# Attention slots of a fused attention and expert kernel: tasks assigned anew, products in halves

## The chip, the cores and the metric

One core of a Trainium2 chip runs the whole program in one launch. The metric is the time of that launch on the device in microseconds, the median of the runs shown.

## The reference, cut to what matters

Input are 8 sequences of 512 rows of 256 values and one condition vector of 64 values for each. First comes a residual attention with 16 heads of 16 channels:

```
qkv  = x @ Wqkv.T + bqkv;  attn = softmax(q k / 4)
coh  = sigmoid(tanh([x, cond] @ Wc1.T + bc1) @ Wc2.T + bc2)
mod  = attn * coh;  mod /= mod.sum(-1) + 1e-8
fa   = softmax(layernorm(relu(cond @ We1.T + be1) @ We2.T + be2) @ pe.T)
x   += (0.79 * mod + 0.21 * fa) @ v @ Wout.T + bout
```

Then a residual mixture of 8 experts with the two best taken for each row: a gate on the normed row, `h1 = relu(x W1 + b1)`, `h2 = relu(h1 W2 + b2)`, `h2 W3 + b3`, weighed by the gate's softmax.

## The kernel before, in words

Each of the 8 sequences (a batch here) goes through 16 slots: 4 groups of 4 heads, and in a group 4 tiles of 128 keys. A slot s has, in TensorE's program (line 1095):

- `scores(s, (0, 1))`: for two heads a `b_tile` (line 877, the S tile: keys by queries, 512 columns, matmul on line 885) and an `a_tile` (line 863, matmul on line 874) of the slot six ahead. VectorE takes the maxima of the a tiles (`reduce_head`, line 1320), ScalarE the exps of the b tiles (`exps`, line 1203). Three PSUM banks go round for a tiles, two for b tiles, so b tile n waits for the exp of b tile n - 2, and a tile n for the maximum of a tile n - 3.
- `pv(s - 1)`: P times V of the slot before, 8 matmuls in fp32 (line 898), 17 columns wide, for four heads side by side; it waits for all four exps of that slot.
- `scores(s, (2, 3))`.
- `product(t)` (line 959) for each task t that PLAN (line 150) names for the slot. A task is (what, index, batches ahead). `pj` (q and k projections), `c1` (the hidden layer of the coherence) and `v` (values with the gate's inputs, line 971) are six fp16 matmuls each, three for each half e of the channels (`thirds`, line 946, matmul on line 950); x and the weights are split in a high and a low part. `coh` is the coherence (line 1008), `vs` the sum of v over all rows (line 1011), `ot` turns a group's result (line 956), `at` turns half of the channels of the finished attention back, `op` is the output projection, `count` numbers the rows for the experts. Two misc banks alternate over the tasks in the order in which they are issued (`USES`); a task waits until the one before the last is evicted.

The other engines run the same slots in the same order, each in its own queue, and nothing overtakes within one:

- ScalarE (line 1257): exps 0 and 1; in slots 0, 4, 8, 12 `copy_out`, and for the batch before `square_rows` (slots 4 to 7), `send_high` (line 1224, slots 8 and 9) and `weigh`; exps 2 and 3; the evictions of the slot's tasks (`take`, line 1153); in slot 4 `split_x` (line 1146) for the batch after next.
- VectorE (line 1653): the maxima, between them the steps of the routing (`ROUTE_AT`), evictions, `send_low` (slots 8 and 10). At 2, 6, 10, 14 `split_maxima` (line 1322) hands a group's maxima to SP's `store_shift`, which the group's b tiles wait for two slots later.
- GpSimd (line 769): `bias_values` of v tasks and `split_projection` of pj tasks in the slot behind theirs; `fade` (slots 2 and 10), `split_x` (5), `sum_values` (line 671, slot 6, what `vs` needs), gate steps, and `scatter` (line 732): eight indirect DMAs a batch that send the rows to their experts, spread by SCATTER_AT over slot 15 and slots 0, 3, 4 and 6 of the next batch.
- SP (line 560): `write_parts` sends a projection's parts to DRAM (slots 10, 12, 14, 15), `read_stacks` fetches them stacked for the next batch (slots 0, 3, 4).

`send_high` and `send_low` write a finished batch's rows, in two fp16 parts, into the one buffer `sent`, from which `scatter` reads. So `send_high` waits for all scatters of the batches before (line 1227):

```
evicted(act, ("op", r.stop - 1, b))
after(act, scattered, 16 * 2 * TT * b)
```

In the first six batches PLAN's projections are for the batch after next; the last batch has none, and there the expert tables and the first experts' weights are made. From 528 us on the experts run.

Of the kernel before, what the change touches and what calls it, by code (L numbers as in the profile page):

```python
# [9 lines left out]
B, S, E = 8, 512, 256  # L10
# [4 lines left out]
ET = E // P  # L15
# [123 lines left out]
def after(engine, semaphore, count):  # L139
# [10 lines left out]
PLAN = {  # L150
    0: [("coh", 0, 0), ("v", 0, 1)],
    1: [("coh", 1, 0), ("ot", 3, -1)],
    2: [("at", 1, -1), ("coh", 2, 0)],
    3: [("coh", 3, 0), ("op", 0, -1)],
    4: [("op", 1, -1)],
    5: [("ot", 0, 0), ("op", 2, -1)],
    6: [("op", 3, -1)],
    7: [("vs", 0, 0), ("c1", 0, 1)],
    8: [("pj", 0, 2)],
    9: [("ot", 1, 0), ("v", 3, 1)],  # L160
    10: [("pj", 2, 2)],
    11: [("at", 0, 0), ("v", 1, 1)],
    12: [("pj", 1, 2), ("count", 0, -1)],
    13: [("ot", 2, 0), ("pj", 3, 2)],
    14: [("v", 2, 1)],
    15: [("c1", 1, 1)],
# [6 lines left out]

SENT_AT = {8: 0, 10: 1}

SCATTER_AT = {15: (31, 0, 1), 0: (32, 1, 2), 3: (35, 2, 4), 4: (36, 4, 6), 6: (38, 6, 8)}

STACKS_AT = {0: 0, 3: 1, 4: 2}
LEAD = 6
# [41 lines left out]


PROJECTIONS = (0, 2, 1, 3)
PARTS_AT = (10, 12, 14, 15)
WRITES = 16 * 2 * len(PARTS_AT)

# [18 lines left out]
def tasks(s):  # L245

    early = [(what, 0, 0) for what in SETUP_PLAN.get(s, [])]
    here = [(what, i, s // SLOTS + ahead) for what, i, ahead in PLAN[s % SLOTS]]
    return early + [t for t in here if 0 <= t[2] < B]

# [43 lines left out]
def model(nc, ctx, dram, sb, banks, xs, parts_dram, out):  # L294
# [182 lines left out]
    def _(sp):  # L477
# [82 lines left out]
        for s in range(FIRST, LAST):  # L560
            b, at = s // SLOTS, s % SLOTS
            for t in shift_task(s):
                store_shift(*t)
            if s == 1 - SLOTS:
                read_first_stacks()
            elif at in STACKS_AT and 0 < b + 1 < B:
                read_stacks(b + 1, STACKS_AT[at])
            if at == 7:
# [5 lines left out]
                if 0 <= b < B:  # L574
                    sp.dma_start(xr[:, :, 0:E], dram["x"][:, b * TT:(b + 1) * TT, :]).then_inc(xr_in, 16)
            if at in PARTS_AT and 0 <= b + 2 < B:
                write_parts(PARTS_AT.index(at), b + 2)
# [56 lines left out]
    def _(pool):  # L634
# [134 lines left out]
        for s in range(FIRST, LAST):  # L769
# [10 lines left out]
            for t in tasks(s - 1):  # L780
                if t[0] == "v":
                    bias_values(t[1], t[2])
            if at == 5 and 0 < b + 2 < B:
                split_x(b + 2)
            if at == 6 and 0 <= b < B:
                sum_values(b)
# [19 lines left out]
            if at == 13 and 0 <= b - 1 < B:  # L806
                weigh_rows(b - 1)
            if at == 14 and 0 <= b - 1 < B:
                targets(b - 1)
# [53 lines left out]
    def _(pe):  # L863
# [94 lines left out]

        def product(t):
            what, i, b = t  # L960
            side, no = USES[t]
            m = misc[side]
            inputs_ready(t)
            after(pe, misc_read[side], no)
            if what in ("pj", "c1"):
                n = "wc1x" if what == "c1" else "wq" if i < ET else "wk"
                f = slice(i % ET * P, (i % ET + 1) * P)
                for e in range(ET):
                    last = thirds(m[:, :], high[n][:, e, f], low[n][:, e, f], x_high[:, b % 2, e, :], x_low[:, b % 2, e, :],
                                  e == 0, e == ET - 1, False)  # L970
            elif what == "v":
                r = slice(i * P, (i + 1) * P)
                for e in range(ET):
                    last = thirds(m[:, 0:VW], high["wv"][:, e, :], low["wv"][:, e, :], x_high[:, b % 2, e, r],
                                  x_low[:, b % 2, e, r], e == 0, e == ET - 1, True)
# [45 lines left out]
            elif what == "count":  # L1021
                marks = both[:, :, :].rearrange("p t e -> p (t e)")
                nc.tensor.matmul(m[:, 0:TT * NX], tri16[:, :], marks, start=True, stop=True, skip_group_check=True)
                for t2 in range(1, TT + 1):
                    last = nc.tensor.matmul(m[:, t2 * NX:(TT + 1) * NX], ones16[:, :], marks[:, 0:(TT + 1 - t2) * NX],
                                            start=False, stop=(t2 == TT), skip_group_check=True)
            last.then_inc(misc_ready[side], 1)

# [66 lines left out]
        for s in range(FIRST, LAST):  # L1095
            scores(s, (0, 1))
            if scored(s - 1):
                pv(s - 1)
            scores(s, (2, 3))
            for t in tasks(s):  # L1100
                product(t)
            if s == FINAL + 14:
                pe.wait_ge(a_read, B * SLOTS * G)
                hold_ranks(0, EARLY)
                hidden(0, 0, 0, rank_of(0), 1)
# [30 lines left out]
    def _(act):  # L1136
# [120 lines left out]
        for s in range(FIRST, LAST):  # L1257
            b, at = s // SLOTS, s % SLOTS
            if s == -18:
                split_weights("wc1x")  # L1260
                split_weights("wv")
            if scored(s):
                exps(s, (0, 1))
            if at % TT == 0 and scored(s - 1):
                copy_out(s - 1)
            if 4 <= at < 8 and 0 <= b - 1 < B:
                square_rows(at - 4, b - 1)
            if at in (8, 9) and 0 <= b - 1 < B:
                send_high(at - 8, b - 1)
            elif at == 10 and 0 <= b - 1 < B:  # L1270
                weigh(b - 1)
            if scored(s):
                exps(s, (2, 3))
            for t in tasks(s):
                take(t)
            if at == 4 and 0 <= b < B:
                act.wait_ge(z_ready, b + 1)
                nc.scalar.activation(ez[:, :, :], z[:, :, :], ACT.Exp, scale=-1.0).then_inc(ez_ready, 1)
            if at == 4 and 0 < b + 2 < B:
                split_x(b + 2)  # L1280
            if s == FINAL + 15:
                take_hidden(0, 0, 0)
            if s in SPLIT_AT:
                split_quarter(*SPLIT_AT[s])
# [523 lines left out]
```

## Time and profile before

| | us |
|---|---|
| median of 3 runs (lowest, highest) | 940.82 (937.77, 941.13) |
| the profiled execution's own time | 950.3 |
| its span, first to last instruction | 948.4 |
| PE, DVE, ACT, POOL busy | 878.1, 699.8, 581.5, 406.3 |
| lead-in until the first S tile | 56.3 |
| eight attention batches | 56.3 to 528.4 |

PE is TensorE, PEld its weight loads, DVE VectorE, ACT ScalarE, POOL GpSimd, SP the engine that issues most DMAs. A line in the rows is the line of the instruction, often that of a helper. Matmuls overlap: an instruction's own length is more than the time until the next can start, so two in a row are compared by their starts.

### The profile page before, as it was taken

How to read it: one execution, taken by the hardware profiler on the slowest of the kernel's cores; microseconds unless marked ns; L12 is line 12 of the kernel's file. 1: busy time of each engine (PE TensorE's matmuls, PEld its weight loads, DVE VectorE, ACT ScalarE, POOL GpSimd, SP SyncE). 2: the span in 40 equal slices, each digit the busy share in tenths (PEclk: the TensorE clock that was granted, in tenths of full speed). 3: DMA queues.
4: the chain of work that ended last, by engine and by line, in shares of the span. 5: the costliest groups of instructions: out<-in, count | busy, mean ns of one | idle time of the engine just before them, and what ended most of it. 6: DMA issues, size and time to landing. Idle time of an engine off the chain costs nothing.

```text
span 948.4 us, 23132 instructions
## 1 busy us (share of the span) xinstructions
PE 878.1 (93%) x6806; PEld 514.9 (54%) x6807; DVE 699.8 (74%) x1680; ACT 581.5 (61%) x1256; POOL 406.3 (43%) x446
## 2 busy tenths in 40 slices
PE   5799999999999999998888989799999999999994
PEld 2232333333333333332231678678888888888873
DVE  6768889888998988989996387768865555555442
ACT  3147877877778878787586657655444444444441
POOL 4313435555646656553253326643553233223322
PEclk9679999999999999999896899989999999999998
DMA  6543243443526426171053187875644333333432
GB/s 207 121 80 71 66 53 91 97 113 79 97 82 109 122 60 127 42 124 48 13 173 114 26 243 179 192 191 100 129 74 57 46 57 52 51 46 55 66 49 25
DMA packets 109434, 88.36 MB, mean 93 GB/s; under 512 B 63816, under 2 KB 102216, under 8 KB 107024
## 3 DMA queue, kind: packets, MB, share of 16 engines
q1 hardware_dynamic: 95664, 68.05, 31.6%
q0 software_dynamic: 13296, 18.23, 11.6%
q8 instruction: 50, 0.82, 0.4%
q10 hardware_dynamic: 384, 0.93, 0.3%
q14 instruction: 40, 0.33, 0.1%
HBM read 44.97 MB, written 33.31 MB: 83 GB/s over the span
## 4 chain that ended last, share of the span: by engine, by line
PE 74%; DVE 11%; ACT 5%; DMA 4%; issue 3%; POOL 1%; SPq 1%; DVEq 0%; ACTq 0%; POOLq 0%
PE bank L1053 30%; PE bank L950 10%; PE bank L898 10%; PE bank L1069 9%; PE bank L885 8%; DVE mx L1320 5%; PE bank L874 4%; ACT arena L1203 2%; PE bank L956 2%; DVE arena L1627 1%; DMA w_b<-mxp 1%; PE bank L1008 1%; DMA out<-y,y_dest 1%; POOL arena L654 1%; ACT arena L1151 1%
## 5 line engine op out<-in xcount | busy, mean ns | idle before, releaser
L1320 DVE TENSOR_REDUCE mx<-bank 128x1 f32<-128x512 f32 x512 | 324.3, 682 | 49.2 <-PE bank L874 46.1
L1203 ACT ACTIVATE arena<-bank 128x512 f32<-128x512 f32 x512 | 277.4, 596 | 70.4 <-PE bank L885 68.5
L1239 ACT ACTIVATE hf<-bank,small 128x256 f32<-128x256 f32 (+1 forms) x312 | 133.5, 456 | 190.2 <-PE bank L1053 188.3
L753 POOL DMA_INDIRECT out<-y,y_dest x71 | 130.5, 1838 | 239.5 <-DVE y_dest L1608 207.8
L1053 PE MATMUL bank<-hh,arena 128*128 128x256 f16 (+1 forms) x1248 | 198.6, 265 | 0.1
L874 PE MATMUL bank<-arena 48*128 48x512 f16 x512 | 170.8, 396 | 16.8 <-DVE mx L1320 12.8
L1589 DVE TENSOR_TENSOR hl<-hf,hh 128x256 f16<-128x256 f32 (+1 forms) x304 | 112.6, 395 | 93.7 <-ACT hh L1243 93.2
L885 PE MATMUL bank<-arena 49*128 49x512 f16 x512 | 164.5, 394 | 14.6 <-DMA arena<-w_b 6.3
L1053 PE MATMUL bank<-hl,arena 128*128 128x256 f16 (+1 forms) x624 | 163.6, 263 | 0.0
L898 PE MATMUL bank<-arena 128*17 128x512 f32 x1024 | 139.6, 618 | 0.9 <-ACT arena L1203 0.9
L885 PEld LDWEIGHTS bank<-arena 49*128 49x128 f16 x512 | 39.1, 94 | 177.5 <-ACT arena L1203 149.2
L1053 PEld LDWEIGHTS bank<-hh,arena 128*128 x1248 | 121.3, 98 | 19.4 <-issue 1.0
L1053 PE MATMUL bank<-x_parts,arena 128*128 128x256 f16 (+1 forms) x936 | 108.6, 273 | 10.2 <-issue 7.8
L1053 PEld LDWEIGHTS bank<-x_parts,arena 128*128 x936 | 88.9, 101 | 25.4 <-issue 12.5
L1069 PE MATMUL bank<-arena,hh 128*128 x568 | 95.5, 273 | 1.6 <-DVE y L1600 1.2
L950 PE MATMUL bank<-arena,raw 128*128 128x512 f16 x288 | 78.9, 417 | 5.7 <-DVE raw L1567 3.5
L1069 PE MATMUL bank<-arena,hl 128*128 x284 | 77.4, 273 | 0.0
L735 POOL DMA_INDIRECT xs<-sent,slot x64 | 66.2, 1034 | 15.4 <-issue 14.4
L1243 ACT ACTIVATE hh<-bank,small 128x256 f16<-128x256 f32 (+1 forms) x156 | 71.6, 459 | 0.0
L1583 DVE CAST hh<-hf 128x256 f16<-128x256 f32 (+1 forms) x156 | 46.6, 323 | 25.0 <-ACT hf L1239 18.7
L1053 PEld LDWEIGHTS bank<-hl,arena 128*128 x624 | 61.2, 98 | 5.6
L1069 PEld LDWEIGHTS bank<-arena,hh 128*128 128x128 f16 x568 | 55.5, 98 | 10.8 <-issue 3.7
(228 smaller groups left out, 971.3 us busy)
## 6 DMA issues: line engine op xcount, KB each, us to landing
raw<-in_we SPq DMA_DIRECT2D x16, 1024.0 KB, 5.2
arena<-parts_dram SPq DMA_DIRECT2D x84, 128.0 KB
parts_dram<-arena SPq DMA_DIRECT2D x64, 128.0 KB, 1.8
arena<-in_xT SPq DMA_DIRECT2D x8, 512.0 KB, 4.5
arena<-in_x SPq DMA_DIRECT2D x8, 512.0 KB, 5.9
out<-rows SPq DMA_DIRECT2D x8, 512.0 KB, 5.2
xs<-in_pads SPq DMA_DIRECT2D x9, 272.0 KB, 3.6
arena<-parts_dram SPq DMA_DIRECT2D x24, 64.0 KB, 3.0
```

Of the source, the lines that this page charges most:

```text
L753: pool.indirect_dma_start(out=out, out_offset=bass.IndirectOffsetOnAxis(ap=y_dest[:, par, s:s + 1], axis=0), in_=y[:, par, s, :], in_offse ...
L874: nc.tensor.matmul(a_bank[no % A_RING][:, :], q[r, par, h // 2, at * P:(at + 1) * P], k[r, par, h // 2, :], start=True, stop=True).then_in ...
L885: nc.tensor.matmul(b_bank[no % B_RING][:, :], k[r, par, h // 2, at * P:(at + 1) * P], q[r, par, h // 2, :], start=True, stop=True).then_in ...
L898: last = nc.tensor.matmul(pv_bank[HW * h:HW * h + SUM + 1, :], v[:, par, jt, g * G + h, :], pr[:, jt, h, :], start=(jt == 0), stop=(jt == ...
L950: done = nc.tensor.matmul(out_ap, a, c, start=(first and n == 0), stop=(last and n == 2), skip_group_check=True)
L1053: last = nc.tensor.matmul(out, weights(name, part, e, k, c), a, start=(k == 0 and n == 0), stop=(k == K - 1 and n == 2), skip_group_check= ...
L1069: last = nc.tensor.matmul(y_bank[:, s * E:(s + 1) * E], a, weights("w3", part, e, k, slice(0, E)), start=(k == 0 and n == 0), stop=(k == M ...
L1203: nc.scalar.activation(pr[:, s % TT, n, :], b_bank[no % B_RING][:, :], ACT.Exp, scale=SCALE).then_inc(b_read, 1)
L1239: nc.scalar.activation(hf[which][:, m, 0:n], layer[which][m // 2][:, m % 2 * TS:m % 2 * TS + n], ACT.Relu, bias=bias[which][:, bass.ds(e, ...
L1243: nc.scalar.activation(hh[1][:, par, m, 0:n], layer[1][m // 2][:, m % 2 * TS:m % 2 * TS + n], ACT.Relu, bias=bias[1][:, bass.ds(e, 1), m], ...
L1320: V.tensor_reduce(mx[:, g % 2, c, s % TT:s % TT + 1], a_bank[no % A_RING][:, :], X, ALU.max).then_inc(a_read, 1)
L1589: nc.vector.tensor_tensor(hl[which][:, par, j, 0:n], hf[which][:, j, 0:n], hh[which][:, par, j, 0:n], ALU.subtract).then_inc(lo[which], 1)
```

## The change

PLAN is reordered: `v 0` goes from slot 0 to 4 and `at 0` from slot 11 to slot 0 of the next batch (in the last batch to slot 13), `vs` from 7 to 6, `v 2` from 14 to 13, `pj 3` from 13 to 14; in slot 9 v stands first. `pj`, `c1` and `v` are issued in halves: the three matmuls of e = 0 behind P times V, those of e = 1 at the task's old place, into the same bank. The waits of a task then stand ahead of its first half. ScalarE's squares go to slots 5 (two), 6 and 7, `send_high` to 6 and 9, `send_low` to 7 and 14, `split_x` to slots 1 (ScalarE) and 2 (GpSimd), `sum_values` to 5, `targets` to 15, the last `write_parts` to slot 0 behind, and the first `read_stacks` to slot 1. SCATTER_AT, ROUTE_AT and the lead of 6 slots stay.

```diff
--- before.py
+++ after.py
@@ -148,21 +148,21 @@
 
 SHIFTS_AT = {14: (0, 1), 2: (1, 0), 6: (2, 0), 10: (3, 0)}
 PLAN = {
-    0: [("coh", 0, 0), ("v", 0, 1)],
+    0: [("at", 0, -1), ("coh", 0, 0)],
     1: [("coh", 1, 0), ("ot", 3, -1)],
     2: [("at", 1, -1), ("coh", 2, 0)],
     3: [("coh", 3, 0), ("op", 0, -1)],
-    4: [("op", 1, -1)],
+    4: [("v", 0, 1), ("op", 1, -1)],
     5: [("ot", 0, 0), ("op", 2, -1)],
-    6: [("op", 3, -1)],
-    7: [("vs", 0, 0), ("c1", 0, 1)],
+    6: [("op", 3, -1), ("vs", 0, 0)],
+    7: [("c1", 0, 1)],
     8: [("pj", 0, 2)],
-    9: [("ot", 1, 0), ("v", 3, 1)],
+    9: [("v", 3, 1), ("ot", 1, 0)],
     10: [("pj", 2, 2)],
-    11: [("at", 0, 0), ("v", 1, 1)],
+    11: [("v", 1, 1)],
     12: [("pj", 1, 2), ("count", 0, -1)],
-    13: [("ot", 2, 0), ("pj", 3, 2)],
-    14: [("v", 2, 1)],
+    13: [("v", 2, 1), ("ot", 2, 0)],
+    14: [("pj", 3, 2)],
     15: [("c1", 1, 1)],
 }
 SETUP_PLAN = {-27: ["cond"], -18: ["wog"], -17: ["fp"], 1: ["fpT"], 2: ["gg"], 3: ["field"], 5: ["fa"]}
@@ -171,11 +171,13 @@
 
 BIAS_AT = {14: 14, 15: 15, 0: 16, 2: 18}
 
-SENT_AT = {8: 0, 10: 1}
+SENT_HIGH_AT = {6: 0, 9: 1}
+SENT_AT = {7: 0, 14: 1}
+SQUARES_AT = {5: (0, 1), 6: (2,), 7: (3,)}
 
 SCATTER_AT = {15: (31, 0, 1), 0: (32, 1, 2), 3: (35, 2, 4), 4: (36, 4, 6), 6: (38, 6, 8)}
 
-STACKS_AT = {0: 0, 3: 1, 4: 2}
+STACKS_AT = {1: 0, 3: 1, 4: 2}
 LEAD = 6
 FIRST, LAST = -28, B * SLOTS
 FINAL = (B - 1) * SLOTS
@@ -220,8 +222,9 @@
     return not isinstance(i, int) or i >= LOWS_FROM[which]
 
 
+HALVED = ("pj", "c1", "v")
 PROJECTIONS = (0, 2, 1, 3)
-PARTS_AT = (10, 12, 14, 15)
+PARTS_AT = (10, 12, 14, 16)
 WRITES = 16 * 2 * len(PARTS_AT)
 
 
@@ -246,6 +249,8 @@
 
     early = [(what, 0, 0) for what in SETUP_PLAN.get(s, [])]
     here = [(what, i, s // SLOTS + ahead) for what, i, ahead in PLAN[s % SLOTS]]
+    if s == FINAL + 13:
+        here.append(("at", 0, B - 1))
     return early + [t for t in here if 0 <= t[2] < B]
 
 
@@ -561,6 +566,8 @@
             b, at = s // SLOTS, s % SLOTS
             for t in shift_task(s):
                 store_shift(*t)
+            if at == PARTS_AT[3] - SLOTS and 0 <= b + 1 < B:
+                write_parts(3, b + 1)
             if s == 1 - SLOTS:
                 read_first_stacks()
             elif at in STACKS_AT and 0 < b + 1 < B:
@@ -573,7 +580,7 @@
                     keep_rows(b - 1)
                 if 0 <= b < B:
                     sp.dma_start(xr[:, :, 0:E], dram["x"][:, b * TT:(b + 1) * TT, :]).then_inc(xr_in, 16)
-            if at in PARTS_AT and 0 <= b + 2 < B:
+            if at in PARTS_AT[:3] and 0 <= b + 2 < B:
                 write_parts(PARTS_AT.index(at), b + 2)
             if s == -1:
                 sp.dma_start(xs[NX * CAP:NX * CAP + TS, :].rearrange("(p r) n -> p r n", r=TS // P),
@@ -780,9 +787,9 @@
             for t in tasks(s - 1):
                 if t[0] == "v":
                     bias_values(t[1], t[2])
-            if at == 5 and 0 < b + 2 < B:
+            if at == 2 and 0 < b + 2 < B:
                 split_x(b + 2)
-            if at == 6 and 0 <= b < B:
+            if at == 5 and 0 <= b < B:
                 sum_values(b)
             if at == 8:
                 if 0 <= b - 1 < B:
@@ -805,7 +812,7 @@
                 mark(b - 1)
             if at == 13 and 0 <= b - 1 < B:
                 weigh_rows(b - 1)
-            if at == 14 and 0 <= b - 1 < B:
+            if at == 15 and 0 <= b - 1 < B:
                 targets(b - 1)
             if at in SCATTER_AT and 0 <= s - SCATTER_AT[at][0] < (B - 1) * SLOTS:
                 scatter(*SCATTER_AT[at][1:])
@@ -956,21 +963,22 @@
                 last = nc.tensor.transpose(m[:, t * P:(t + 1) * P], src(t), w["ident"][:, :])
             return last
 
-        def product(t):
+        def product(t, es=range(ET)):
             what, i, b = t
             side, no = USES[t]
             m = misc[side]
-            inputs_ready(t)
-            after(pe, misc_read[side], no)
+            if es[0] == 0:
+                inputs_ready(t)
+                after(pe, misc_read[side], no)
             if what in ("pj", "c1"):
                 n = "wc1x" if what == "c1" else "wq" if i < ET else "wk"
                 f = slice(i % ET * P, (i % ET + 1) * P)
-                for e in range(ET):
+                for e in es:
                     last = thirds(m[:, :], high[n][:, e, f], low[n][:, e, f], x_high[:, b % 2, e, :], x_low[:, b % 2, e, :],
                                   e == 0, e == ET - 1, False)
             elif what == "v":
                 r = slice(i * P, (i + 1) * P)
-                for e in range(ET):
+                for e in es:
                     last = thirds(m[:, 0:VW], high["wv"][:, e, :], low["wv"][:, e, :], x_high[:, b % 2, e, r],
                                   x_low[:, b % 2, e, r], e == 0, e == ET - 1, True)
             elif what == "cond":
@@ -1024,7 +1032,8 @@
                 for t2 in range(1, TT + 1):
                     last = nc.tensor.matmul(m[:, t2 * NX:(TT + 1) * NX], ones16[:, :], marks[:, 0:(TT + 1 - t2) * NX],
                                             start=False, stop=(t2 == TT), skip_group_check=True)
-            last.then_inc(misc_ready[side], 1)
+            if es[-1] == ET - 1:
+                last.then_inc(misc_ready[side], 1)
 
         def weights(name, part, e, k, cols):
             first, width = LAYERS[name]
@@ -1096,9 +1105,12 @@
             scores(s, (0, 1))
             if scored(s - 1):
                 pv(s - 1)
+            for t in tasks(s):
+                if t[0] in HALVED:
+                    product(t, range(ET // 2))
             scores(s, (2, 3))
             for t in tasks(s):
-                product(t)
+                product(t, range(ET // 2, ET) if t[0] in HALVED else range(ET))
             if s == FINAL + 14:
                 pe.wait_ge(a_read, B * SLOTS * G)
                 hold_ranks(0, EARLY)
@@ -1263,10 +1275,11 @@
                 exps(s, (0, 1))
             if at % TT == 0 and scored(s - 1):
                 copy_out(s - 1)
-            if 4 <= at < 8 and 0 <= b - 1 < B:
-                square_rows(at - 4, b - 1)
-            if at in (8, 9) and 0 <= b - 1 < B:
-                send_high(at - 8, b - 1)
+            if at in SQUARES_AT and 0 <= b - 1 < B:
+                for t in SQUARES_AT[at]:
+                    square_rows(t, b - 1)
+            if at in SENT_HIGH_AT and 0 <= b - 1 < B:
+                send_high(SENT_HIGH_AT[at], b - 1)
             elif at == 10 and 0 <= b - 1 < B:
                 weigh(b - 1)
             if scored(s):
@@ -1276,7 +1289,7 @@
             if at == 4 and 0 <= b < B:
                 act.wait_ge(z_ready, b + 1)
                 nc.scalar.activation(ez[:, :, :], z[:, :, :], ACT.Exp, scale=-1.0).then_inc(ez_ready, 1)
-            if at == 4 and 0 < b + 2 < B:
+            if at == 1 and 0 < b + 2 < B:
                 split_x(b + 2)
             if s == FINAL + 15:
                 take_hidden(0, 0, 0)
```

## Rows read from the trace of the kernel before

**Rows 1.** stages: us, busy us (and instructions) of PE, PEld, DVE, ACT, POOL, granted clock, DMA
```profile
288.70:346.00 57.30, 55.77 (x390) 20.08 (x391) 51.70 (x110) 45.87 (x93) 32.98 (x44) 1.00 0.44 98
...
402.90:463.20 60.30, 54.04 (x366) 18.69 (x367) 54.56 (x126) 43.03 (x88) 25.76 (x37) 0.94 0.36 74
463.20:528.40 65.20, 54.56 (x316) 18.27 (x315) 46.94 (x105) 42.30 (x83) 22.24 (x31) 0.82 0.33 107
```

**Rows 2.** the same for one batch, cut at first S tiles of slots
```profile
288.71:302.04 13.33, 13.05 (x101) 5.60 (x101) 11.51 (x24) 10.61 (x20) 6.35 (x7) 1.00 0.51 109
302.04:309.37 7.33, 6.65 (x50) 2.44 (x50) 6.30 (x14) 6.48 (x15) 5.20 (x6) 1.00 1.13 134
309.37:312.62 3.25, 3.23 (x23) 1.03 (x23) 3.22 (x8) 2.55 (x6) 2.71 (x4) 1.00 0.39 95
312.62:320.15 7.53, 7.53 (x47) 2.34 (x47) 6.55 (x13) 5.99 (x13) 4.26 (x6) 1.00 0.56 173
320.15:327.27 7.12, 7.12 (x50) 2.53 (x50) 6.74 (x15) 5.92 (x13) 3.90 (x5) 1.00 0.25 83
327.27:335.61 8.34, 7.79 (x54) 2.65 (x53) 7.96 (x24) 6.36 (x13) 2.89 (x5) 1.00 0.19 63
335.61:345.97 10.36, 10.36 (x74) 3.46 (x71) 9.43 (x21) 7.96 (x15) 7.68 (x13) 1.00 0.13 39
```

**Rows 3.** timeline of TensorE: start, us, line, tiles, count, idle time before
```profile
38.28 0.61 PE L874 MATMUL bank<-arena 48*128 48x512 f16 x1 [0.36 <-DVE mx L1320]
...
313.16 1.05 PE L898 MATMUL bank<-arena 128*17 128x512 f32 x8
314.14 0.39 PE L885 MATMUL bank<-arena 49*128 49x512 f16 x1
...
314.68 0.70 PE L1011 MATMUL bank<-hh,x_parts 128*128 128x256 f32 x2
315.22 1.46 PE L950 MATMUL bank<-arena,raw 128*128 128x512 f16 x6
316.61 0.39 PE L885 MATMUL bank<-arena 49*128 49x512 f16 x1
...
329.41 0.66 PE L956 MATMUL bank<-small,arena 128*128 128x128 f32 x4
329.90 0.86 PE L950 MATMUL bank<-raw,arena 128*128 128x272 f16 x6
330.69 0.39 PE L885 MATMUL bank<-arena 49*128 49x512 f16 x1
```

**Rows 4.** timeline of ScalarE, slots 4 to 8
```profile
305.69 1.06 ACT L1151 ACTIVATE arena<-arena 128x1024 f16<-128x1024 f32 x1
...
310.82 0.42 ACT L1207 ACTIVATE squared<-rows 128x256 bf16<-128x256 f32 x1
...
314.57 1.08 ACT L1203 ACTIVATE arena<-bank 128x512 f32<-128x512 f32 x2
316.71 0.69 ACT L1164 ACTIVATE arena<-bank,cbias 128x512 f32<-128x512 f32 x1 [1.06 <-PE bank L950]
...
318.76 0.62 ACT L1228 ACTIVATE sent<-rows 128x512 f16<-128x512 f32 x1
```

**Rows 5.** timeline of VectorE, slot 12
```profile
331.70 0.68 DVE L1394 TENSOR_TENSOR arena<-bank,arena 128x512 f16<-128x512 f32 x1
```

**Rows 6.** timeline of GpSimd, slots 5, 6 and 10
```profile
308.92 1.11 POOL L674 TENSOR_TENSOR hh<-arena 128x512 f32<-128x512 f32 x1
...
310.99 1.02 POOL L735 DMA_INDIRECT xs<-sent,slot  x1 [0.15 <-issue]
312.32 0.97 POOL L735 DMA_INDIRECT xs<-sent,slot  x1 [0.30 <-issue]
...
324.15 0.71 POOL L669 TENSOR_TENSOR arena<-arena,w_b 128x272 f32<-128x272 f32 x1 [1.09 <-ACT arena L1171]
```

**Rows 7.** GB/s that the DMA engines moved, 310 to 316 us, 40 slices
```profile
GB/s 116 145 232 232 116 58 109 0 0 0 0 0 0 32 171 15 0 377 377 174 1 0 0 0 0 203 290 406 29 0 0 0 0 14 0 0 0 12 2 0
```

## The prediction

> **What bounds the kernel now.** I read the busy time by stage first: from 56 to 403 us six batches of the attention follow each other; in the one that stands in the rows, 57.3 us long, TensorE is busy 55.77, VectorE 51.70, ScalarE 45.87, GpSimd 32.98 [rows 1]. TensorE is the bound, but VectorE has under 6 us to spare in a batch. The next two batches (60.3 and 65.2 us) have no projections of a later batch left; there the granted clock is 0.94 and 0.82 against 1.00, and table building and weight splitting take turns [rows 1]. The expert stage behind is not touched.
>
> Then one batch by slots. A slot starts with its first S tile (line 885). Slots 7, 8, 9, 10 and 13 to 15 leave TensorE no visible idle time; slots 4 and 5 lose 0.68 us, slots 11 and 12 0.55 us, where VectorE is busy 7.96 of 8.34 us [rows 2]. The busy figure hides short stalls, so I also took slot lengths from the starts of the S tiles: with what a slot must issue (below), the stalls sum to about 4 us a batch, 1.5 in slots 4 to 6, 1.5 in slot 12, the rest in small ones. That is all that reordering can win.
>
> Last the timeline of a slot. Slot 7 opens at 312.62 [rows 2]; P times V starts at 313.16 and the second pair of S tiles at 314.14, 0.98 later; the sum of v takes 0.54; six projection matmuls start at 315.22, and the next slot opens at 316.61, 1.39 later [rows 3]. So a slot costs 2.06 us and its products: 1.40 a projection or c1, 0.79 a v product (329.90 to the S tile at 330.69), 0.49 a transposition of att (from 329.41) [rows 3]. The exps of a pair of S tiles start 0.43 us after the pair (314.57 against 314.14) and take 1.08 [rows 3, 4]. The ring for them has two banks, so the second S tile of the next pair can't go before about 1.57 us have passed since this pair.
>
> **The change part by part**, for a batch from the third on (57.26 us before, [rows 2]), slot by slot.
>
> Halves. A halved product puts one half behind P times V and one at the end. Matmuls stay the same in number, but there is one more passage between kinds of matmul in a slot. Its price is not shown for this pair of kinds. Nearest row: six matmuls in 1.46 us, the last 0.39 long, are 0.214 apart, the last starts at 316.29, and the next S tile comes 0.32 after it: 0.11 more than the pace [rows 3]. Nothing issues less, so below nothing is excluded; bounds are 0 and 0.2, and I take 0.11. The Trainium skill (TensorEngine Tiling (Array Packing), Key Properties) says that a change of tiling mode drains TensorE; by that P times V to product pays as S to product does, and the 0.11 stands, without it the sum below would be about 0.9 us a batch smaller. In a slot that ends with a half projection, the last pair of S tiles now stands 0.54 + 0.75 before the next slot, whose second S tile comes at 1.52 and wants 1.57: 0.05 us each.
>
> Slots 0 to 3 (13.33). v 0 leaves (0.80), at 0 comes (0.49): 13.0. But at 0 has a VectorE subtraction of 0.68 [rows 5] which first waits for ScalarE's copy; behind it in VectorE's queue stand coh 0, the maxima of slot 1, the evict of ot 3, and for that GpSimd's fade and at 1 wait. Bounds: 0 (VectorE idles 1.8 us here, 11.51 busy of 13.33 [rows 2]) and the 0.68 twice; I take 0.5: 13.5. ScalarE's x split (1.06, [rows 4]) moves to the end of slot 1, where 10.61 of 13.33 is busy [rows 2]: hidden.
>
> Slots 4 and 5 (7.33). The x split behind slot 4 and the squares and copy in front of it made the exps late; 1.08 us of stall by the starts of S tiles. With the split gone these go; the two squares in slot 5 fit between its exps. v 0 comes with 0.80 and 0.11: 7.33 - 1.08 + 0.91 = 7.15.
>
> Slot 6 (3.25). Without its 0.41 stall and with the sum of v: 3.4, 3.5 with VectorE a little late. **Here the change adds a wait.** send_high of the first half now stands in slot 6 (line 1224), ahead of exps 2 and 3. It overwrites the buffer `sent`, so it waits for all eight scatters of the batch before; the last two are issued by GpSimd in slot 6 itself (SCATTER_AT is unchanged). Before, it came at 318.76, long after [rows 4]. GpSimd must first, in slot 5, add the bias of v 0 (0.71), which is evicted only at the end of slot 4, and sum v (308.92 to the scatter's start at 310.99, 2.07); then two scatters from 310.99 to 313.29, 2.30 [rows 6]; the last bytes move in the slice that ends at 314.35, 1.0 us later [rows 7]. Completion can be later still; I bound it by 1.0 and 1.6 and take 1.4. From slot 5's start: 0.6 (gate values, evict) + 0.71 + 2.07 + 2.30 + 1.4 = 7.1, slot 5 takes 3.35, so 3.75 after slot 6 starts. ScalarE is there at 1.9: two exps from 0.48, then a square of some 0.5 [rows 4]. It waits 1.85, copies (0.62, [rows 4]), and exp 2 ends near 5.0; the first S tile of slot 7 needs its bank, 1.5 later than at 3.5, and the second waits 0.25 more. Queued behind it on ScalarE: exps 2, 3; on TensorE all of slot 7. Cost 1.8, between 1.0 (ScalarE itself late by 0.5, quick landing) and 2.3. Slot 6: 5.05.
>
> Slots 7 and 8 (7.53): without the sum of v, with two passages, two times 0.05 and the 0.25: 7.4. The evict of a product (0.69) precedes the next exps [rows 4]; in a halved slot P times V and a half cover that, which takes off 0.1.
>
> Slots 9 and 10 (7.12): about 0.3 of small stalls go, two passages come: 7.05. send_low moves to slots 7 and 14 and leaves VectorE here.
>
> Slots 11 and 12 (8.34), VectorE bound: at's subtraction leaves, 0.68 or 0.60 at pace [rows 5], the routing steps stay; TensorE's part, 6.4, is no limit. 7.75.
>
> Slots 13 to 15 (10.36, all TensorE): three passages less 0.05: 10.65. VectorE's added send_low fits (9.43 busy [rows 2]).
>
> Sum: 13.5 + 7.15 + 5.05 + 7.4 + 7.05 + 7.75 + 10.65 = 58.55, 1.3 more than 57.26. Four batches (third to sixth) have it all: +5.2. The second waits for no scatter: -0.5. The first, without rows to send: 0. The seventh has the wait and four v and two c1 halves, while VectorE's gain is taken back by send_low before the tables: +1.8. The eighth: +1.0, as its slot 6 was already 4.1 long. The stretch up to 56.3 us: pj 3 now goes behind the product of wo, half a us later in the parts; but maxima no longer hold up the fourth score tile (0.36 idle, in each of six slots, [rows 3]; a half product now stands in between): -1.4, between -2.4 and +1. The queues of SP: the last part is written at slot 0 rather than 15, and its stacks are read from slot 1; they are wanted in slot 10, so this is free.
>
> Total +6.1 on the profiled execution's 950.3 (span 948.4 and 1.9 around it): 956.4. It ran 1.0% above the median of the three, 940.82; on that I get **946.8**.
>
> **The rivals.**
> *The scatter is no hindrance* (faster). Place: send_high in slot 6. If the last scatter lands by 1.9 us after slot 6 opens, 1.85 us earlier than I work out, the 1.8 go in six batches: 10 us less, about 936; with passages free, 932. For it: GpSimd has 24 us a batch idle [rows 1]. Against: v 0's evict is late in slot 4, and 5 us of GpSimd's work stand behind it. It decides from a wait of some 0.8 us down: there the gains, 0.5 a batch and 1.4 ahead, take over. 0.24.
> *The gains and the wait cancel* (no change). Passages free, or VectorE catches up during the wait, so that slot 12 needs 0.5 less: 0.9 less a batch, 941. For it: VectorE loses its lag in slot 6. Against: it falls behind anew from slot 9 on. 0.21.
> *ScalarE late at the second half* (slower). Second gap of a halved slot is 0.75 where it was 1.4; if the exps come 0.2 late there, all of it is lost, seven times a batch: +1.4, 9 us in all, 955. Against: ScalarE idles 11 us a batch [rows 1]. 0.12.
> *The halves don't do what they say*: the bank of a first half must be free half a slot earlier. By the order of tasks its last user was evicted a slot before in every case, so I see no wait; 0.03, within the range.
>
> **How the numbers follow.** Forecast 0.40, 946.8, own range 942 to 953. A measurement can tell 0.5%, 4.7 us, from no change. Faster (below 936.1): most of the first rival, 0.23. Same (to 945.5): the second, the low end of the forecast, some of the first: 0.33. Slower: 0.44. Range 934 to 955: beyond it some 0.1 of the first rival and 0.06 of the third.
>
> **What would show it.** Right: in slot 6 of batches 3 to 7 send_high's copy on ScalarE is preceded by 1.5 to 2 us of idle time for the scatter, and slot 6 lasts about 5 us; slots 4 and 5 without stalls; slots 11 and 12 near 7.75; VectorE's idle time gathered in slot 6. Passages: six matmuls of a halved projection with 1.50 us between their neighbours instead of 1.39. Wrong: no wait at that line, or one under 0.8 us; slots 11 and 12 at 6.5; or idle time of TensorE at the first S tiles of every slot behind a projection.

## The result, and the profile after

The changed kernel takes 964.81 us (median of 4 runs, 962.38 to 969.16) against 940.98 for the kernel before (4 runs): ratio 1.0251, 95% interval 1.0187 to 1.0314. Its profiled execution took 965.5 us with a span of 963.5, 15.1 more than the span before. So it is slower by 23.8 us where the forecast said 5.8, and outside the range. Medians are over all executions, ratios leave out those over 1.5% above the fastest of their kernel.

Batches are counted from 0 in what follows and in the expectations; the rows of before show batch 4 [rows 1, 2]. In after, the windows of batch 4 and of the two last batches (columns as in [rows 1]):

```profile
291.80:354.14 62.34, 58.21 (x389) 19.27 (x389) 51.31 (x111) 45.49 (x94) 33.37 (x45) 0.97 0.41 89
416.12:477.81 61.69, 55.10 (x364) 18.15 (x365) 53.13 (x123) 42.74 (x89) 26.65 (x38) 0.94 0.35 73
477.81:545.50 67.69, 56.35 (x320) 18.90 (x321) 48.63 (x111) 42.68 (x84) 24.46 (x33) 0.82 0.33 105
```

And batch 4 cut at the first S tiles of the same slots as in [rows 2]:

```profile
291.80:305.53 13.73, 13.39 (x101) 5.83 (x100) 12.48 (x26) 11.73 (x22) 8.60 (x9) 1.00 0.49 101
305.53:313.91 8.38, 7.21 (x56) 2.94 (x56) 5.98 (x13) 5.93 (x15) 5.69 (x8) 1.00 1.12 157
313.91:319.63 5.72, 3.52 (x25) 1.38 (x25) 4.26 (x12) 2.66 (x8) 2.29 (x3) 1.00 0.22 74
319.63:328.69 9.06, 8.96 (x44) 1.81 (x45) 5.21 (x9) 5.96 (x13) 3.60 (x5) 0.81 0.57 175
328.69:335.72 7.03, 7.03 (x49) 2.20 (x49) 5.99 (x14) 5.74 (x13) 3.95 (x5) 1.00 0.03 7
335.72:343.54 7.82, 7.50 (x51) 2.01 (x51) 7.44 (x22) 6.08 (x13) 2.89 (x5) 1.00 0.20 68
343.54:354.14 10.60, 10.60 (x75) 3.11 (x72) 9.95 (x22) 7.40 (x15) 6.35 (x12) 1.00 0.08 24
```

| slots | before | predicted | after |
|---|---|---|---|
| 0 to 3 | 13.33 | 13.5 | 13.73 |
| 4, 5 | 7.33 | 7.15 | 8.38 |
| 6 | 3.25 | 5.05 | 5.72 |
| 7, 8 | 7.53 | 7.4 | 9.06 |
| 9, 10 | 7.12 | 7.05 | 7.03 |
| 11, 12 | 8.34 | 7.75 | 7.82 |
| 13 to 15 | 10.36 | 10.65 | 10.60 |
| batch | 57.26 | 58.55 | 62.34 |

Four rows of seven came out within 0.25 us. The loss of 5.1 us stands in slots 4 to 8, and there the granted clock is 0.81 in one row. By the starts of the S tiles, batches 2 to 5 together are 18.6 us longer than before, batch 1 is 1.65 shorter.

**Slot 6 and what follows.** The timeline of ScalarE (L1207 is the copy of a P times V result, L1240 `send_high`):

```profile
309.17 0.60 ACT L1207 ACTIVATE w_b<-bank 128x512 f32<-128x512 f32 x1 [1.63 <-remote]
...
318.46 0.63 ACT L1240 ACTIVATE sent<-rows 128x512 f16<-128x512 f32 x1 [2.59 <-DMA xs<-sent,slot]
```

The predicted wait is there, 2.59 us long. TensorE's timeline from the end of slot 6 to the opening of slot 9 (L1019 the sum of v, L892 and L881 the S and a tiles, L905 P times V, L957 a half projection):

```profile
316.84 0.59 PE L1019 MATMUL bank<-hh,x_parts 128*128 128x256 f32 x2
319.63 0.39 PE L892 MATMUL bank<-arena 49*128 49x512 f16 x1 [2.20 <-ACT arena L1215]
...
320.44 1.81 PE L905 MATMUL bank<-arena 128*17 128x512 f32 x8
322.18 1.46 PE L957 MATMUL bank<-arena,raw 128*128 128x512 f16 x3
...
326.64 0.82 PE L957 MATMUL bank<-arena,raw 128*128 128x512 f16 x3
327.40 0.39 PE L892 MATMUL bank<-arena 49*128 49x512 f16 x1
...
327.94 0.82 PE L957 MATMUL bank<-arena,raw 128*128 128x512 f16 x3
328.69 0.39 PE L892 MATMUL bank<-arena 49*128 49x512 f16 x1
```

TensorE idles 2.20 us, until ScalarE's exps free a bank for its S tile; then P times V lasts 1.81 where it took 1.05 [rows 3], and three matmuls 1.46 where the next slot's take 0.82. The windows of single microseconds show why (first number behind the busy times: granted clock):

```profile
319.00:320.00 1.00, 0.37 (x2) 0.10 (x2) 0.00 (x0) 1.00 (x3) 0.00 (x0) 1.00 0.02 2
320.00:321.00 1.00, 0.90 (x8) 0.23 (x10) 0.91 (x2) 0.95 (x3) 0.00 (x0) 0.80 0.02 2
321.00:322.00 1.00, 1.00 (x8) 0.00 (x0) 0.38 (x1) 0.59 (x3) 0.23 (x2) 0.50 1.02 141
...
324.00:325.00 1.00, 1.00 (x7) 0.21 (x3) 0.77 (x2) 0.80 (x2) 1.00 (x1) 0.99 1.10 389
```

Behind the idle stretch TensorE's clock falls to the lower of its two levels, 1.2 instead of 2.4 GHz, and comes back within slot 7. The trace shows such a stretch of 3.4 us from 187.5, 259.2, 320.6, 382.0 and 443.5 us on, one in each of batches 2 to 6 (batch 6 has another from 474.2); before has none between 71 and 449. In batches 3 to 6 it stands behind the wait of slot 6. In batch 2 it stands earlier, in slot 5, behind an idle stretch of 1.96 us in slot 4, where the exps were late for another reason (below):

```profile
186.66 0.39 PE L892 MATMUL bank<-arena 49*128 49x512 f16 x1 [1.96 <-ACT arena L1215]
```

```profile
186.66:191.82 5.16, 5.06 (x27) 1.73 (x28) 3.54 (x9) 3.72 (x11) 3.79 (x5) 0.67 0.63 95
```

There slot 5 takes 5.16 us against 3.60 in batch 4, and `send_high` then waits only 0.78.

**Slot 4.** GpSimd's timeline: the split of x (L644), now in slot 2, and the six scatters (L742) behind it:

```profile
301.05 2.15 POOL L644 TENSOR_TENSOR arena<-arena 128x1024 f16<-128x1024 f32 x1
...
304.04 0.99 POOL L742 DMA_INDIRECT xs<-sent,slot  x1
305.34 0.96 POOL L742 DMA_INDIRECT xs<-sent,slot  x1 [0.30 <-issue]
...
306.95 1.06 POOL L742 DMA_INDIRECT xs<-sent,slot  x1 [0.18 <-issue]
308.32 0.98 POOL L742 DMA_INDIRECT xs<-sent,slot  x1 [0.31 <-issue]
...
314.34 1.03 POOL L742 DMA_INDIRECT xs<-sent,slot  x1
315.67 0.97 POOL L742 DMA_INDIRECT xs<-sent,slot  x1 [0.30 <-issue]
```

VectorE's first maximum behind them, and TensorE's P times V and S tiles of slot 4:

```profile
309.91 1.29 DVE L1333 TENSOR_REDUCE mx<-bank 128x1 f32<-128x512 f32 x2 [2.24 <-remote]
```

```profile
306.50 0.61 PE L905 MATMUL bank<-arena 128*17 128x512 f32 x4
...
307.50 0.60 PE L881 MATMUL bank<-arena 48*128 48x512 f16 x2
```

ScalarE's copy needs only P times V, by its rows over at 307.1, but starts at 309.17; VectorE needs the a tile of 307.50 and starts at 309.91. "remote" is a signal whose sender the profile doesn't name; in the trace TensorE's signals arrive together at 309.15 to 310.09. So slot 4 takes 4.79 us, and 5.67, 5.06 and 4.32 in batches 2, 3 and 5, where scatters and the split both fall; in batches 1 and 6, which have only one of the two, 3.64.

### The profile page after: what moved, and what is told of

It reads as the page before. It is cut to its first block, busy times and chain, and to the rows that moved or that the text cites. A ratio compares the mean times of both kernels' runs of the same rounds, so it can differ in the third digit from the quotient of the medians.

```text
span 963.5 us, 23132 instructions
## 1 busy us (share of the span) xinstructions
PE 888.9 (92%) x6806; PEld 508.5 (53%) x6807; DVE 700.9 (73%) x1680; ACT 579.4 (60%) x1256; POOL 412.6 (43%) x446
## 4 chain that ended last, share of the span: by engine, by line
PE 66%; DVE 10%; issue 6%; ACT 6%; POOL 5%; DMA 4%; SPq 1%; another core or an unknown queue 0%; ACTq 0%; DVEq 0%; POOLq 0%
PE bank L1062 29%; PE bank L1078 9%; PE bank L957 8%; PE bank L905 8%; PE bank L892 6%; DVE mx L1333 5%; ACT arena L1215 3%; PE bank L881 3%; POOL xs L742 2%; DMA xs<-sent,slot 1%; PE bank L963 1%; PE bank L1016 1%; POOL arena L661 1%; DMA out<-y,y_dest 1%; POOL arena L676 1%
## 5 line engine op out<-in xcount | busy, mean ns | idle before, releaser
L760 POOL DMA_INDIRECT out<-y,y_dest x71 | 132.7, 1869 | 234.7 <-DVE y_dest L1621 198.8
L892 PE MATMUL bank<-arena 49*128 49x512 f16 x512 | 167.9, 400 | 24.2 <-ACT arena L1215 16.5
L881 PE MATMUL bank<-arena 48*128 48x512 f16 x512 | 172.5, 400 | 11.7 <-DVE mx L1333 6.1
L905 PE MATMUL bank<-arena 128*17 128x512 f32 x1024 | 143.3, 633 | 0.9 <-ACT arena L1215 0.9
L892 PEld LDWEIGHTS bank<-arena 49*128 49x128 f16 x512 | 38.5, 94 | 156.2 <-ACT arena L1215 105.2
L1062 PE MATMUL bank<-x_parts,arena 128*128 128x256 f16 (+1 forms) x936 | 104.6, 267 | 10.9 <-issue 10.8
L1062 PEld LDWEIGHTS bank<-x_parts,arena 128*128 x936 | 86.9, 99 | 24.3 <-issue 12.9
L957 PE MATMUL bank<-arena,raw 128*128 128x512 f16 x288 | 84.4, 410 | 3.6 <-DVE raw L1580 2.7
L742 POOL DMA_INDIRECT xs<-sent,slot x64 | 66.8, 1043 | 20.5 <-issue 12.5
L957 PEld LDWEIGHTS bank<-arena,raw 128*128 128x128 f16 x288 | 22.2, 102 | 73.0 <-issue 59.0
```

Source lines behind the costliest of these rows:

```text
L742: pool.indirect_dma_start(out=xs, out_offset=bass.IndirectOffsetOnAxis(ap=slot[:, i, t:t + 1], axis=0), in_=sent[:, t, :], in_offset=None) ...
L760: pool.indirect_dma_start(out=out, out_offset=bass.IndirectOffsetOnAxis(ap=y_dest[:, par, s:s + 1], axis=0), in_=y[:, par, s, :], in_offse ...
L881: nc.tensor.matmul(a_bank[no % A_RING][:, :], q[r, par, h // 2, at * P:(at + 1) * P], k[r, par, h // 2, :], start=True, stop=True).then_in ...
L892: nc.tensor.matmul(b_bank[no % B_RING][:, :], k[r, par, h // 2, at * P:(at + 1) * P], q[r, par, h // 2, :], start=True, stop=True).then_in ...
L905: last = nc.tensor.matmul(pv_bank[HW * h:HW * h + SUM + 1, :], v[:, par, jt, g * G + h, :], pr[:, jt, h, :], start=(jt == 0), stop=(jt == ...
L957: done = nc.tensor.matmul(out_ap, a, c, start=(first and n == 0), stop=(last and n == 2), skip_group_check=True)
```

## The experiments

Ratios are against the kernel before on the same chip, 29 executions of it in each of three sets, with medians of 942.64 (experiments 1 to 4), 943.56 (5 and 6) and 943.81 (7 to 9). A name in brackets is that of the kernel; the expectations use it.

**1. `send_high` where it was** (`late_send`).

```diff
-SENT_HIGH_AT = {6: 0, 9: 1}
-SENT_AT = {7: 0, 14: 1}
+SENT_HIGH_AT = {8: 0, 9: 1}
+SENT_AT = {8: 0, 14: 1}
```

> The kernel after with ScalarE's copy of the rows to be sent back in slots 8 and 9 (VectorE's part in 8 and 14). Theory (the wait for the scatters in slot 6, and behind it TensorE's clock at half for 3.4 us): slot 6 falls from 5.7 to about 3.4 and slot 7 from 5.4 to about 3.6 in batches 3 to 6, some 4 us a batch, 18 us in all: about 947. Rival (slot 7 is long because of its halved product, not because of the stall before it): only slot 6 gets shorter, 2.3 a batch, about 955. Rival (the wait hides other lateness that comes out elsewhere): under 5 us, 960 or more. Slot 4 stays at 4.3 to 5.7 by all of them.

948.05, ratio 1.0053 (1.0020 to 1.0085). Its windows of slot 6 and of slots 7 and 8:

```profile
309.97:313.34 3.37, 3.37 (x27) 1.38 (x26) 3.30 (x9) 2.55 (x7) 2.26 (x3) 1.00 0.21 69
313.34:320.53 7.19, 7.19 (x46) 1.64 (x46) 5.48 (x11) 5.97 (x13) 3.60 (x5) 1.00 0.49 145
```

From 14.78 to 10.56 us in three slots, and no low clock in batches 1 to 5: the first theory, by its numbers. Four fifths of the loss, by the ratios 1.0251 and 1.0053, are this one move.

**2. The wait kept, TensorE kept busy in it** (`fill`).

```diff
-                last = nc.tensor.matmul(m[:, 0:E], ones[:, :], vpart[:, :], start=True, stop=True)
+                for _ in range(4 if 2 <= b < 7 else 1):
+                    last = nc.tensor.matmul(m[:, 0:E], ones[:, :], vpart[:, :], start=True, stop=True)
```

> The kernel after with the sum of v issued four times instead of once in slot 6 of batches 2 to 6 (the same values in the same bank), about 1.6 us of TensorE work inside the wait of slot 6; nothing else is moved. Theory (the idle time of TensorE makes its clock fall to half in slot 7): slot 6 stays near 5.7, the granted clock stays at 1.00 in slot 7, which falls from 5.4 to 3.9; 1.5 us in each of four or five batches, about 958. Rival (slot 7 is late for want of exps or because of the halved product): no gain, 965 or a little more.

959.18, ratio 1.0167 (1.0122 to 1.0212). That is 0.8% under the ratio of after, but the two intervals overlap; firmer are the profiles of both, where batches 2 to 5 together take 245.1 us against 248.9, by adding work (the two profiles of before differ by 0.8 there). Slot 6, then slots 7 and 8:

```profile
313.51:319.16 5.65, 4.96 (x31) 2.48 (x30) 4.49 (x12) 2.63 (x7) 2.22 (x3) 1.00 0.17 59
319.16:327.32 8.16, 7.73 (x44) 1.81 (x44) 6.43 (x8) 6.19 (x13) 3.59 (x5) 1.00 0.63 196
```

The clock stays at 1.00 from 68 to 464 us, and slot 7 falls from 5.44 to 3.84, while ScalarE still waits 2.52 for the scatters. So the low clock is the price of TensorE's idleness, not of the halves. Slot 8 took 0.7 back: VectorE's `send_low` lasted 2.22 us there instead of 0.68 beside a GpSimd operation of 1.90 (experiment 5 has the reason).

**3. The scatters of slots 3 and 4 earlier** (`late_send_split`). GpSimd's split goes behind them:

```diff
-            if at == 2 and 0 < b + 2 < B:
-                split_x(b + 2)
...
+            if at == 7 and 0 < b + 2 < B:
+                split_x(b + 2)
```

> As late_send, and GpSimd's split of x from slot 2 to slot 7, behind the scatters of slot 6, so that the scatters of slots 3 and 4 start some 2 us earlier. Theory (slot 4 loses its 0.7 to 2 us in batches 2 to 5 because these scatters run beside P times V of slot 4): slot 4 falls to the 3.64 that batches 1 and 6 have, 5 us less than late_send: about 942. Rival (slot 4 is long because of the halved v product or of the stack reads): slot 4 as in late_send, the same time as late_send.

947.10, ratio 1.0030 (0.9989 to 1.0071). Slots 4 and 5, then 7 and 8 of batch 4:

```profile
300.76:307.73 6.97, 6.97 (x56) 2.79 (x56) 6.05 (x13) 6.04 (x15) 5.16 (x7) 1.00 1.13 139
...
311.11:319.26 8.15, 7.20 (x45) 1.59 (x45) 5.48 (x11) 6.14 (x13) 4.77 (x6) 1.00 0.41 116
```

Slot 4 is 3.64 in batches 1 to 6, with the v product still halved: the split ahead of the scatters made it long. Batches 2 to 5 are 4.4 us shorter together. But in batch 4 1.0 us came back in slot 7 (1.6 in batch 2): the maxima of the next group landed late, as in before's batch 2 (5.54 there). And in batches 0 and 1, where there are no scatters to hold it back, the split ran beside VectorE's scaling of the maxima, and slot 6 took 4.16 and 4.25 instead of 2.88 and 3.37 (experiment 5 has the reason). By the medians the gain is within the noise.

**4. Halves alone, in the old plan** (`old_plan_halves`). `product` and its two calls as in the change, PLAN as before.

> The kernel before, with its own plan, and the projection, c1 and v products in halves; nothing else. Theory as predicted (a passage more in each of nine slots a batch at 0.11): 1 us a batch, 7 in all, about 948. Rival (passages are free, and the halves take off small stalls): 938 to 941. Rival (ScalarE late at the second pair): 950 or more, idle time of TensorE at the first S tiles behind projections.

942.89, ratio 0.9991 (0.9953 to 1.0029). Its batch 4:

```profile
278.06:336.20 58.14, 56.47 (x388) 18.86 (x388) 51.11 (x111) 45.79 (x94) 33.24 (x45) 1.00 0.43 92
```

58.14 against 57.26: 0.9 a batch, near the 1 us expected, but not made up as expected. There are ten halved products, and slots 7, 13 and 14 are 0.10 to 0.11 longer; of the rest slot 15 alone has 0.38. Its first two S tiles:

```profile
332.36 0.39 PE L886 MATMUL bank<-arena 49*128 49x512 f16 x1
...
332.85 0.39 PE L886 MATMUL bank<-arena 49*128 49x512 f16 x1
```

They stand 0.49 apart instead of 0.23: behind the short second half of a v product the exps that free the bank come 0.26 late. That is the third rival in small. The total shows nothing of the 0.9; this profile's lead-in was short (batch 1 at 103.65, before 114.25).

**5. Scatters and split spread out** (`spread`). GpSimd's split in slot 6, the last scatters in slot 7.

```diff
+            if at == 6 and 0 < b + 2 < B:
+                split_x(b + 2)
...
-SCATTER_AT = {15: (31, 0, 1), 0: (32, 1, 2), 3: (35, 2, 4), 4: (36, 4, 6), 6: (38, 6, 8)}
+SCATTER_AT = {15: (31, 0, 1), 0: (32, 1, 2), 3: (35, 2, 4), 4: (36, 4, 6), 7: (39, 6, 8)}
```

> As late_send, with GpSimd's split of x in slot 6 and the last two scatters in slot 7 instead of 6, so that the four scatters of slots 3 and 4 start early and the last two no longer run beside the transposing transfer of the maxima in slot 6. Theory (scatters beside other transfers are what made slots 4 and 7 long): slot 4 at 3.64 and slot 7 at 3.57 in every batch from the third on, a batch of 56.7 us in the profile, 0.5 less than before has: 3 us less than late_send_split, about 944. Rival (slot 7 was long there because the split of x stood in it): slot 7 at 3.57 too, but slot 8 or 9 longer by what the scatters now delay, no gain over late_send_split.

948.39, ratio 1.0030 (0.9998 to 1.0063). Slot 4 at 3.64 and slot 7 at 3.57 (4.94 in batch 2) as expected, but slot 6 takes 4.24. VectorE's scaling of the maxima there, and GpSimd's split:

```profile
307.75 1.03 DVE L1339 TENSOR_SCALAR mxp<-mx 128x16 f16<-128x16 f32 x1
```

```profile
306.62 2.14 POOL L644 TENSOR_TENSOR arena<-arena 128x1024 f16<-128x1024 f32 x1
```

An operation that takes 0.16 us elsewhere lasts 1.03 and ends with the split (308.78 and 308.76), and all maxima queue behind it. The Trainium skill (SBUF — State Buffer, Who interferes with whom) states such an exclusive lock, on a pair of memory ports that the two engines share, held for the whole instruction; the trace agrees. I had not looked for it.

**6. Whole products.** `spread` with halves only for `s < 0` (`spread_lead`) and with `HALVED = ()` (`spread_whole`), and the kernel before with halves only for `s < 0` (`old_plan_lead_halves`).

> As spread, with halves only in the slots ahead of the first batch; from there on the products are whole. Theory (each halved slot costs a passage of about 0.1, as old_plan_halves shows in slots 7, 13 and 14): 0.8 us a batch less than spread, six batches, 5 us less: about 939. Rival (in the new order the halves cover ScalarE's evictions and exps): the slots behind a whole projection get a stall of 0.1 to 0.3 and the time is that of spread or more.

950.52, ratio 1.0103 (1.0071 to 1.0135): a miss. Slots 4 and 7 to 10 are 0.45 shorter in sum, but slots 13 to 15 are 0.2 longer and slot 6 is 4.70; the batch 57.7 (58.4 in batch 4), no shorter than in `spread`. In slot 6 VectorE's scaling now meets more of GpSimd's split (1.52 us in batch 3 instead of 1.03); outside slot 6 whole products took 0.3 us off batch 3. So the test of the halves was mixed with the lock.

> As spread, with no halves anywhere. Against spread_lead it tells what the halves do in the lead-in. Theory (there they keep TensorE busier while the maxima are taken): the first S tile some 5 us later than in spread_lead, and the time 4 to 6 us longer, about 944. Rival (the lead-in is set by the projections' way through DRAM): the same time as spread_lead.

955.19, ratio 1.0118 (1.0071 to 1.0165). The first S tile comes 6.5 us later than in `spread_lead`, but batch 1 only 1.2. By the medians it is 4.7 us longer, as expected; the intervals overlap, and the two profiles (949.2 and 951.6) don't show it.

> The kernel before with halves only in the slots ahead of the first batch. Theory (halves cost 0.9 us in a batch of the old plan and gave that back in the lead-in): batches as before (57.3), the lead-in as in old_plan_halves: 5 to 6 us under the kernel before, about 937. Rival (the lead-in of old_plan_halves was short in its one profile only, for the clock there): the time of the kernel before, 942 to 943.

944.07, ratio 0.9982 (0.9941 to 1.0023): no change to measure, though its profile reached batch 1 at 105.6.

**7. The kernel before, a second profile** (`before_again`).

> The kernel before, unchanged, for a second profile of it. Theory (the lead-in and the first batch differ from execution to execution with the stretches at half clock): the first S tile of the second batch comes anywhere from 104 to 114 us, while the third to the sixth batch take 57.3 each as in the first profile. Rival (the lead-in of the kernel before always takes 114): 114 again, and then the shorter lead-ins of the kernels with halves are their own.

936.06 us. Its lead-in, batch 0 and batch 4, and behind them the lead-in and batch 0 of the first profile:

```profile
0.00:49.21 49.21, 33.30 (x133) 14.08 (x135) 38.47 (x68) 13.78 (x25) 22.52 (x37) 0.90 0.58 159
49.21:105.64 56.43, 54.63 (x370) 19.25 (x370) 46.34 (x90) 42.95 (x82) 19.82 (x23) 1.00 0.39 81
...
278.69:336.01 57.32, 55.78 (x388) 20.05 (x388) 51.71 (x110) 45.91 (x93) 33.01 (x44) 1.00 0.44 97
```

```profile
0.00:56.27 56.27, 37.78 (x132) 14.24 (x134) 38.58 (x68) 13.77 (x25) 22.67 (x37) 0.82 0.57 153
56.27:114.25 57.98, 56.49 (x369) 19.30 (x369) 46.24 (x90) 42.93 (x82) 19.81 (x23) 0.96 0.34 66
```

Same instructions, 8.6 us apart at batch 1; 10.2 us at the low clock against 23.9. Batch 4 agrees to 0.1, batches 3 and 5 to 0.2 and 0.4, batch 2 only to 1.3 (57.51 and 58.84). So lead-ins of single profiles can't be compared to better than 8.6 us. Whether experiment 4's short one is a merit of the halves stays open: in all profiles together the first S tile comes at 46.3 to 50.4 us with halves ahead of batch 0 and at 49.2 to 56.3 without them, while the median of `old_plan_lead_halves` shows no gain.

**8. The change mended** (`mended`). `late_send`; GpSimd's split in slot 6, held until the scaled maxima are out, the last scatters behind it; whole products from batch 0 on; the old plan ahead of it.

```diff
+            if at == 6 and 0 < b + 2 < B:
+                if b >= 0:
+                    pool.wait_ge(mx_split, b * NG + 3)
+                split_x(b + 2)
```

> The kernel after with the three things mended that the runs so far name: the copy of the rows to be sent back in slots 8 and 9; GpSimd's split of x in slot 6, started only when VectorE's scaled maxima are out, with the last scatters behind it; products whole from the first batch on, and the order of the old plan with halves ahead of it. Theory: slot 4 at 3.54, slot 6 at 3.4 instead of spread_lead's 4.7, a batch of 56.4 against 57.3 before, lead-in as in old_plan_lead_halves; 5 us under the kernel before, about 938. Rival (the last two batches, where the new plan lost 3 to 5 us at the half clock in every profile, take it back): 942 to 945.

941.52, ratio 0.9991 (0.9963 to 1.0018). Slots 4 and 5, and slot 6, of batch 3:

```profile
235.15:242.08 6.93, 6.93 (x56) 2.94 (x56) 6.09 (x14) 5.82 (x15) 4.79 (x7) 1.00 1.15 136
242.08:245.39 3.31, 3.31 (x26) 1.41 (x26) 3.28 (x8) 2.67 (x7) 2.48 (x2) 1.00 0.52 101
```

The batch is 56.31 (57.02 in batch 4), and the whole is level with before, as the rival had it. Batches 6 and 7, up to the last slot, take 130.5 us together against 125.6 and 123.5 in the two profiles of before. Eight profiles of the new plan have 127.0 to 133.5 there (mean 129.8), six of the old plan 123.5 to 129.2 (mean 126.0). So a loss of some 4 us is likely; that it is the low clock is not shown, for the time at it overlaps (30.7 to 37.5 us, 20.5 to 41.0).

**9. Two edits of the change in the old plan.** ScalarE's split in slot 1 and `SQUARES_AT = {5: (0, 1), 6: (2,), 7: (3,)}` (`old_scalar`); then with halves ahead of batch 0 as well (`old_scalar_lead`).

> The kernel before with two of the change's edits alone: ScalarE's split of x in slot 1 instead of 4, and the squares in slots 5 (two), 6 and 7. Theory (as predicted for slots 4 and 5: these two made the exps late there, 1.08 us): slots 4 to 6 fall from 10.6 to about 9.4, 1.1 a batch over five batches, 937. Rival (VectorE or GpSimd is late there as well): under 0.4 a batch, no change to measure.

943.09, ratio 0.9994 (0.9960 to 1.0027). Slots 4 to 6 of batch 3, in before and here:

```profile
244.77:255.34 10.57, 9.89 (x71) 3.47 (x72) 9.50 (x21) 9.03 (x21) 7.89 (x9) 1.00 0.92 122
```

```profile
241.63:251.20 9.57, 9.51 (x71) 3.54 (x71) 9.13 (x21) 8.20 (x20) 7.92 (x9) 1.00 0.98 137
```

They fall by 1.0, near the 1.1 expected, but slot 7 is 5.5 in batches 2 and 4 (the maxima's transfer again), and the total shows no gain.

> As old_scalar, and halves in the slots ahead of the first batch. Theory (halves there keep TensorE busier, so that less of the lead-in is at half clock): 3 to 5 us less than old_scalar. Rival (old_plan_lead_halves was no faster than the kernel before by its median): the same as old_scalar.

937.27, ratio 0.9936 (0.9894 to 0.9978), the fastest of the changed kernels and 0.6% under the kernel before. Its lead-in with batch 0, and batch 4:

```profile
0.00:104.48 104.48, 88.43 (x500) 33.05 (x502) 85.25 (x158) 56.77 (x107) 42.44 (x60) 0.95 0.47 119
274.94:331.29 56.35, 55.56 (x388) 20.05 (x388) 51.37 (x110) 45.80 (x93) 32.99 (x44) 1.00 0.44 99
```

How much of that is the halves' can't be told: its interval overlaps that of `old_scalar`.

## Why the prediction was wrong

*Slot 6: the right wait, mis-sized, and cut off too early.* ScalarE waited for the last two scatters as forecast, 2.59 us instead of 1.85 in batch 4. Of the difference, the landing makes 0.4: `send_high` starts 1.82 us behind the end of the second scatter (316.64), where the last bytes in the DMA traffic [rows 7] had led me to 1.4, at most 1.6. The Trainium skill (Perfetto Trace Analysis, DMA Instruction — SWDGE (GPSIMD)) says that such a record ends with the descriptors, not with the data; 1.82 is what came behind it here. The other 0.4 is GpSimd, late behind slot 4 (in `late_send_split`, with slot 4 short, its scatters start 0.3 earlier in slot 6). The step that failed is the next one: "on TensorE all of slot 7", priced at the wait alone. The idle 2.20 us cost the clock as well, 1.6 to 1.9 us in slot 7 (5.44 against 3.84 in `fill` and 3.57 in `late_send`), nearly as much again. I had read clocks of 0.94 and 0.82 in the last batches and of 1.00 here [rows 1], and took 1.00 as given. Slots 7 and 8 came out 1.66 over the forecast. Experiments 1 and 2 show both parts.

*Slots 4 and 5: a queue not read.* ScalarE's split and squares did make the exps late (10.57 to 9.57, experiment 9), by 1.0 where 1.08 in slots 4 and 5 and 0.41 in slot 6 were forecast. But I priced only ScalarE's half of the moved split. GpSimd's half, 2.15 us, moved ahead of the scatters of slots 3 and 4 in its queue; slots 4 and 5 came out 1.2 over the forecast in batch 4, and with it behind them they take 6.97 (experiment 3). In batch 2 this wait cost the clock as well. What holds TensorE's signals while these scatters run beside the stack reads is open: no run here isolates the cause. Holes in the record don't tell either: of the 512 signals of S tiles the trace of after holds 487 and that of before 511, but the second profile of before holds 478, and its slot 4 has no such late starts.

*Halves.* The passage was right: six halved matmuls stand 0.76 and 0.75 us before their neighbours (326.64 to 327.40, 327.94 to 328.69), 1.51 where 1.50 was forecast and 1.39 measured whole. The 0.9 a batch in the old plan is partly luck: a third of it is a wait for exps in slot 15 (experiment 4). In the new plan whole products took 0.3 off a batch outside slot 6 (experiment 6).

*Slots 0 to 3 and 9 to 15.* Right to 0.25 us, the VectorE-bound slots 11 and 12 to 0.07.

*Lead-in and ends.* Forecast -1.4 up to batch 1 and +2.8 for the last two; the profiles gave -3.7 and +3.8, and -2.0 behind them. Experiment 7 shows that the first is inside what one kernel does by itself. The 3.8 in batches 6 and 7 is what the means of the two plans' profiles differ by (experiment 8); its cause stays open.

*From span to median.* I carried over that the profile of before stood 1.0% above its median, as if it were a factor. It was for the most part one slow lead-in: of the 14.3 us by which its span exceeds that of the second profile, 8.6 stand ahead of batch 1. After's profile stands at its median. So of the 18 us missing in the forecast, 9 stand in the profile (+15.1 against +6.1: batches 2 to 5 cost 13.4 more than forecast, and the rest 4.4 less), and 9 are this scaling.

## What to carry to other kernels

Price a new wait with what TensorE's clock does behind it: here an idle stretch of some two microseconds in each of four batches cost almost twice its length, and filling it with useless matmuls was faster, by the profiles, than leaving it empty. When a step moves, look up its second half on the other engines, and everything queued behind it there. Compare steady stages, not lead-ins, and take a second profile of the unchanged kernel before reading one or two per cent out of a single one.

## What the runs showed that was not expected

VectorE's scaling of the maxima, 0.16 us by itself, lasted 0.20 to 1.66 us where a GpSimd operation held it, and then ended within 0.04 us of that operation; one that started just ahead of a GpSimd operation kept its 0.16. A computing operation that had clearly begun and had more than 0.16 us left held it every time, the issue of a scatter only in some cases. And one unchanged kernel took from 935 to 953 us (one execution of 1379 apart), and in its two profiles 10 and 24 us of the first 75 were at the low clock.
